# A three-layer decoder block on one core: VectorE's chains cut into single steps, and every engine's call list written anew

## The reference, cut to what matters

```python
x = _layernorm(x + attn(x))            # a state-space mixer: x @ W_in, a 4-tap causal
                                       # convolution, silu, decay matrices, gate, W_out
x = _layernorm(x + xattn(ctx, x))      # 8 heads of 64; keys are the 120 context rows
                                       # and the 256 own rows, 376 in all
x = _layernorm(x + ffn(x))

def ffn(x):
    gf = global_net(x.mean(axis=1, keepdims=True))
    out = x
    for _ in range(3):
        tf = coupling_net(out)         # three gelu layers and a sigmoid
        coupling = 0.1 + adaptive_range * (0.7 * gf + 0.3 * tf - 0.5) * 2
        out = out + coupling * twist(out)
    return out
```

## Time and profile before

| | |
|---|---|
| median of 3 runs | 3865.07 us (3864.32 to 3865.35) |
| span of the profiled execution | 3861.4 us |
| device time of the profiled execution | not given apart from the span; the span lies 3.7 us under the median |
| TensorE busy | 3783.3 us, 98% |
| VectorE busy | 3286.2 us, 85% |
| ScalarE busy | 3237.9 us, 84% |
| GpSimd busy | 1748.5 us, 45% |
| transfers | 203.14 MB, mean 53 GB/s |

### The profile page before, as it was taken

One profiled execution on the slowest core, in us unless ns is written; L12 is line 12 of the kernel. 1 busy time (PEld: TensorE's weight loads), 2 busy tenths in 40 slices (PEclk: granted clock), 3 DMA queues, 4 the chain that ended last, 5 costly groups with the idle time before them and its releaser, 6 DMA issues.

```text
span 3861.4 us, 77375 instructions
## 1 busy us (share of the span) xinstructions
PE 3783.3 (98%) x25728; PEld 3000.9 (78%) x25728; DVE 3286.2 (85%) x8098; ACT 3237.9 (84%) x7812; POOL 1748.5 (45%) x3084
## 2 busy tenths in 40 slices
PE   6999999999999999999999999999999999999997
PEld 5777877877877878778778778777787787787775
DVE  7888888888888888888888888888888888888874
ACT  5788888888888888888888888888888888888885
POOL 3444445354454444453544544534535445445442
PEclk8999999999999999999999999999999999999998
DMA  3111112111211111121111111111211211111110
GB/s 97 54 47 59 55 45 61 54 42 58 58 45 55 48 59 54 45 61 53 43 57 59 45 55 50 56 55 45 61 55 42 61 55 45 55 54 53 55 38 17
DMA packets 312350, 203.14 MB, mean 53 GB/s; under 512 B 55056, under 2 KB 310928, under 8 KB 311952
## 3 DMA queue, kind: packets, MB, share of 16 engines
q1 hardware_dynamic: 311952, 198.20, 17.5%
HBM read 180.17 MB, written 17.96 MB: 51 GB/s over the span
## 4 chain that ended last, share of the span: by engine, by line
PE 59%; ACT 16%; DVE 15%; issue 4%; POOL 4%; DMA 1%; SPq 0%; DVEq 0%; POOLq 0%
PE psum L253 20%; PE psum L428 8%; PE psum L338 6%; PE psum L463 5%; PE psum L438 5%; PE psum L452 4%; PE psum L325 4%; ACT prob L979 3%; ACT h L1021 2%; ACT L979 2%; ACT L1021 2%; PE psum L497 2%; ACT xc L891 2%; POOL rs_mix L2175 2%; DVE nmax L1638 1%
## 5 line engine op out<-in xcount | busy, mean ns | idle before, releaser
L979 ACT ACTIVATE prob<-psum,nmax 128x376 f32<-128x376 f32 x1024 | 585.2, 575 | 49.5 <-DVE nmax L1638 46.2
L1638 DVE TENSOR_REDUCE nmax<-psum 128x1 f32<-128x376 f32 x1024 | 541.5, 540 | 14.4 <-PE psum L428 11.0
L2139 POOL TENSOR_TENSOR Lm<-Lm,G 128x384 f32<-128x384 f32 x512 | 506.1, 1012 | 92.8 <-DVE out_sb L1741 68.4
L438 PE MATMUL psum<-ident,prob 128*128 128x128 f32 (+1 forms) x3072 | 480.5, 276 | 2.1 <-ACT probT L989 1.1
L1442 DVE SCALAR_TENSOR_TENSOR u<-psum,par,u 128x253 f32<-128x253 f32 (+5 forms) x960 | 449.1, 479 | 28.1 <-ACT u L882 1.7
L428 PE MATMUL psum<-kT,q_sb 64*128 64x376 f32 x2048 | 467.7, 528 | 0.2 <-ACT prob L979 0.2
L438 PEld LDWEIGHTS psum<-ident,prob 128*128 128x128 f32 (+1 forms) x3072 | 363.0, 141 | 73.9 <-issue 45.0
L989 ACT ACTIVATE probT<-psum 128x384 f32<-128x384 f32 x512 | 252.7, 494 | 182.7 <-PE psum L438 182.5
L2126 POOL TENSOR_SCALAR_AFFINE_SELECT Lm<-Lm 128x256 f32<-128x256 f32 x512 | 205.7, 435 | 411.6 <-DMA Lm<-cum_row 411.6
L253 PE MATMUL psum<-x_hi,w_in_hi 128*128 128x256 f32 (+1 forms) x1152 | 360.9, 313 | 22.5 <-DVE w_in_lo L1764 9.3
L452 PE MATMUL psum<-probT,V 128*64 128x256 f32 (+1 forms) x3072 | 375.0, 385 | 0.3 <-ACT probT L989 0.3
(11 more groups left out here) (222 smaller groups left out, 11157.9 us busy)
## 6 DMA issues: line engine op xcount, KB each, us to landing
Lm<-cum_row SPq DMA_DIRECT2D x64, 1024.0 KB, 5.2
Lm<-cum_row SPq DMA_DIRECT2D x64, 512.0 KB, 6.5
invT<-inv_row SPq DMA_DIRECT2D x256, 128.0 KB, 3.0
xT_sb<-in_xT SPq DMA_DIRECT2D x64, 256.0 KB, 3.1
x_sb<-in_x SPq DMA_DIRECT2D x64, 256.0 KB, 3.3
result<-out_sb SPq DMA_DIRECT2D x64, 256.0 KB, 2.2
inv_row<-inv_t SPq DMA_DIRECT2D x512, 1.0 KB
ctx_sb<-in_ctx SPq DMA_DIRECT2D x64, 120.0 KB, 2.7
```

Of the source, the lines that this page charges most:

```text
L438: t = tr(banks[b][0:m, j * P:(j + 1) * P], prob[:, r, j0:j0 + m], ident[:, :])
L979: act(prob[:, r, :], b[:, 0:NK], ACT.Exp, bias=nmax[:, n:n + 1], accum_out=psum_row[:, n:n + 1]).then_inc(a_exp, 1)
L1638: e.tensor_reduce(nmax[:, n:n + 1], banks[bank_of["sc", s, n]][:, 0:NK], AX.X, ALU.max, negate=True).then_inc(d_max, 1)
L2139: t = tt(Lm[:, h, :], Lm[:, h, :], G[:, :], ALU.mult)
```

## The change

All five engines' lists are drawn up anew, for the prologue, the loop and the tail. The instructions that compute are the same, and as many on TensorE. On VectorE the helpers that held several dependent steps are divided into helpers of one step each, and steps of different chains alternate: `taps` becomes `tap`, `bc` becomes `bc_silu`, `bc_high` and `bc_low`, `cum` three calls, `x1_raw` three calls per half, `kv_split`, `x2_split`, `inverse`, `norm`, `cycle` and `out_sum` likewise. The convolution gets one semaphore for each of its four row blocks in place of one. The bank of `bcdt` is now freed by two semaphores in place of one. The core of it:

```diff
-            def taps(src, c, rows, done, at):
-                for n, d in enumerate((1, 2, 3)):
+            def tap(src, c, rows, n, done, s):
+                d = n + 1
+                ve.wait_ge(done, 3 * s + n)
                     stt(u[0:rows, c, d:L], src[:, 0:L - d], prm("conv_w", 4 * c + 3 - d, slice(0, rows)),
                         u[0:rows, c, d:L], ALU.mult, ALU.add).then_inc(done, 1)
-                    if n < 2:
-                        ve.wait_ge(done, at + n + 1)
...
-                freed[b] = [(d_dta, s + 1)]
+                freed[b] = [(d_dta, s + 1), (d_uB, 3 * s + 3)]
...
-                freed[b] = [(d_u, 12 * s + 6 * j + 6)]
+                freed[b] = [(d_u[2 * j], 3 * s + 3), (d_u[2 * j + 1], 3 * s + 3)]
...
-            def out_sum(s, i):
+            def out_x(s, i):
...
+            def out_tw(s, i, k):
...
-            def cycle(s, cyc):
+            def gain(s, cyc):
...
+            def twisted_part(s, cyc):
...
+            def pre(s, cyc):
```

More of the change, by code:

```diff
@@ L573, in _ @@
+            k_tile(0, 0)
+            k_tile(0, 1)
+            scores(0, 0, 0)
+            xcT(1, 0)
+            in_z(1, 0)
+            k_tile(0, 2)
+            xcT(1, 1)
+            v_tile(0, 0)
+            scores(0, 0, 1)
+            cb(1)
             in_z(1, 1)
             q_pair(0, 1)
[L575 to L581 removed]
             turn(0, 0)
+            scores(0, 1, 0)
@@ L739, in _ @@
+            x1T(last)
+            twisted(last - 2)
             turn(last - 1, 8)
+            layer(last - 2, 0, 3)
+            glob(last - 2, 2)
             turn(last - 1, 9)
-            glob(last - 2, 2)
-            twisted(last - 2)
-            turn(last - 1, 10)
-            x1T(last)
-            layer(last - 2, 0, 2)
+            scores(last - 1, 3, 0)
+            values(last - 1, 0)
+            values(last - 1, 1)
             scores(last - 1, 3, 1)
-            layer(last - 2, 0, 3)
@@ L772, in _ @@
+            values(last - 1, 2)
+            values(last - 1, 3)
+            scores(last, 0, 1)
+            v_tile(last, 0)
+            layer(last - 2, 2, 3)
+            w_o(last - 1, 0)
+            w_o(last - 1, 1)
+            scores(last, 1, 0)
+            turn(last, 0)
             q_pair(last, 1)
-            layer(last - 2, 2, 3)
+            scores(last, 1, 1)
             turn(last, 1)
-            scores(last, 1, 1)
+            x2_turn(last - 1)
+            k_tile(last, 3)
+            scores(last, 2, 0)
@@ L776, in _ @@
             turn(last, 2)
+            v_tile(last, 1)
+            scores(last, 2, 1)
             turn(last, 3)
-            scores(last, 2, 0)
-            k_tile(last, 3)
             turn(last, 4)
-            scores(last, 2, 1)
-            x2_turn(last - 1)
-            v_tile(last, 0)
+            glob(last - 1, 0)
+            layer(last - 1, 0, 0)
+            v_tile(last, 2)
+            scores(last, 3, 0)
             turn(last, 5)
-            glob(last - 1, 0)
-            scores(last, 3, 0)
```

1804 lines of the change are left out of this document (1048 added, 756 removed).

## The result

| | before | after |
|---|---|---|
| median | 3864.7 us (3864.0 to 3865.35) | 4159.2 us (4152.5 to 4163.5, 4 runs) |
| ratio | | 1.076, 95% interval 1.0744 to 1.0775 |
| span of the profiled execution | 3861.4 us | 4161.6 us (device time 4163.5 us) |

The kernel after takes 295 us more. The forecast was 3842 us, its range 3808 to 3880.

A forecast was written before the change was run, and what follows sets the result against it. TensorE, busy 3783.3 of 3861.4 us, was taken as the bound. Loop -0.4 us per iteration times 61 = -24.4, start +3, end -1 gave 3839 us of span; with 3.7 added, 3842 us was forecast, range 3808 to 3880.

The forecast's parts named there:

- term 3: New TensorE waits in the loop, mainly turn(a, 0) behind x2_raw: +0.5 us per iteration (0 to +1.4).
- term 2: TensorE waits in the loop that go, for a gelu, x_lo and small overruns: -0.45 us per iteration (0 to -0.85).
- new waits outweigh: Rival: x2_raw behind the output sums delays TensorE, up to 1.4 us per iteration; 3885 to about 3897 us; chance 0.14.
- Term 1: TensorE's array shape in the loop: four fewer whole-to-half round trips, three more direct half changes, -0.45 us per iteration.
- a wait behind `x2_raw` over 0.9 us: Sign that the forecast is wrong: TensorE's wait behind x2_raw exceeds 0.9 us.
- a gelu's wait that grew: Sign that the forecast is wrong: TensorE's wait for a gelu at the layers grows; no size given.
- Term 4: VectorE's alternating single steps save it some 3 us of 51 per sequence, but 0 of kernel time, TensorE being the bound.
- Term 5: The start: weights and context load placed differently delay the first xcT some 6 us; steady pipeline +3 us (-3 to +8).
- Term 6: The end, one sequence's chain in the last 62 us: -1 us (-3 to +3).
- The eighth table load: Rival: ScalarE's added 1.28 us load before a layer's gelu leaves TensorE waiting; 3858 to 3901 us; chance 0.03.

The follow-up runs named there:

- Experiment 6: Kernel after with VectorE's bc_high, bc_low and x1_keep (2.4 us) moved from ahead of pre to behind it: 4120.0 us, ratio 1.0658 to the kernel before.
- Experiment 1: Kernel after with GpSimd's factors of the output sum no longer waiting for the next sequence's division: 4052.5 us, ratio 1.0487 to the kernel before.
- experiment 9: Kernel before with only the convolution taps of two row blocks alternating, a semaphore for each block: 3861.6 us, ratio 0.9992.
- experiment 2: Kernel after with GpSimd's twist call ahead of the four masked calls instead of behind them: 4123.5 us, ratio 1.0667 to the kernel before.
- Experiment 7: Kernel after with the factors not waiting for the division, and bc_high, bc_low and x1_keep behind pre: 4021.4 us, ratio 1.0402 to the kernel before.
- experiment 12: About 50 loop calls moved to other places by a calculation, in each kernel: before 3876.5 us (1.0034), after 4054.6 us (1.0488).
- experiment 11: Kernel after with the prologue's weights(0, 3) and weights(0, 4) late and SP's context load early, as before the change: 4154.8 us, ratio 1.075 to the kernel before.
- experiment 5: Kernel after with four edits: factors free of the division, twist before masks, spread_inv before loads, two decays behind the copies of oT: 4086.6 us, ratio 1.0576.

## Why the prediction was wrong

**The step that failed is term 3, waits that come: +0.5 per iteration, at most 1.4.** Over the 60 full distances between `x2_turn` calls TensorE is idle for 4.5 us per iteration in place of 0.3: 4.2 us more. Three things in the step were wrong.

*It looked at the wait in the place where I found one, and not at the list in front of each use.* The largest wait stands at `layer(f, 2, 1)`, for which term 2 said that TensorE's cover was "about as much as now" and gave a gain of 0.1. What I didn't add up was VectorE's list between the last copy and `pre`: 11.1 us, and 1.1 more to the gelu's result, against 9.1 us of work on TensorE. Had `bc_silu` taken its old 0.8 us in place of 3.0, 10.0 us would still have stood against 9.1. Experiment 6 shows the cause of this wait: take 2.4 us out, and 109 us of it are gone. The new lists had it all; I counted what TensorE has ahead of its wait, but not what VectorE has ahead of its answer.

*The chain behind the division was the right one, its length and its start were not.* From the second division to `x2_raw` I had 5.2 us; measured 2433.14 - 2427.01 = 6.1. The wait came where it was put (59 times), with 1.04 us in place of 0.35: the chain was 0.9 us longer, 0.97 and 0.74 us for steps that I had at 0.35, beside GpSimd. The forecast's bound (0.8) was passed. And the division itself waits 5.0 us on VectorE, for the sums and for ScalarE, which moves VectorE's whole list. Experiment 1 puts the factors' wait for the division at 107 us, 1.75 us per iteration, 66 of them idle time. The rival "new waits outweigh" named this mechanism, and its point of 0.95 us was passed (by its own sum it is 1.0: 0.9 for terms 1 and 2, 0.1 to pass 3872.8), but its upper price, 1.4, was a third of the 4.2 that came, and more than half of that stands at places that it does not name. Two of the prediction's signs of being wrong came with it: a wait behind `x2_raw` over 0.9 us, and a gelu's wait that grew.

*Prices that depend on a neighbour were taken as fixed.* VectorE's busy time was to fall to 3100 us and rose to 3310: the steps saved by alternating (32 us for the taps, experiment 9) are less than what `bc_silu` alone gained beside GpSimd (58.7 + 85.0 us for its two lines where they took 26.1 + 26.7). The wait at `xcT` (0.87 us per iteration) is due to this; it went when `twist` did (experiment 2). The lower clock behind a stall, some 0.7 us per iteration, was in no term.

The rest by its own steps. **Term 1**, -0.45: too large. Experiment 7 has TensorE's list of after with the lower clock nearly gone. Over the 60 full distances between `x2_turn` calls TensorE is busy for 58.7 us per sequence before, 59.2 after, and 58.5 in experiment 7. The gain is about 0.2 us, near my lower bound. A round trip costs more (0.39) than I took (0.15), so four fewer would be 1.6; that only 0.2 of it is seen would mean, as an estimate, that each of the 3 more changes from one kind of half to the other costs about 0.45, where I took 0.05, or that other costs of the order make up for it. By these two prices the orders of experiment 12 (2 round trips more and 1 direct change fewer, each against its own kernel) should cost 0.3 us; measured were 0.5 and 1.4. So the shapes account for most of the first and for little of the second; what the rest is stays open. **Term 2**: the 4.0 us at `x_lo` went, as said (it waits once, at the start); the gelu's 0.19 became 1.85. **Term 4**, nothing: right, measured at 0.9992. The prediction set the page "VectorE: DVE Perf Modes" of the Trainium skill (The DRAIN you can't avoid) against its rows. Experiment 9 bears the rows out, 2.42 us in place of 2.94 for six taps; and the section says too that a next operation which isn't held starts earlier, so read in full it isn't against them. **Term 5**, +3 with bounds to +8: measured 11.8. Its step at `xcT` was right (7.6 us later where it had 6, and due to the weights and the context load, experiment 11); what it left out is the order of the other calls. **Term 6**, -1: measured +1, in its bounds. **The eighth table load**: ScalarE's busy time rose to 3321 us (3316 forecast), and no wait of TensorE stands at the layer behind it.

The sum, from what was measured: 4.2 idle + 0.7 lower clock (59.2 - 58.5) - 0.2 shapes (58.7 - 58.5) = 4.7 us per iteration, against 4.75 seen. Halving the 89 us at the lower clock gives much the same for the second term, 44 us or 0.8 per iteration.

**What stays open.** With two edits, 138 of 295 us are taken back; at that point TensorE still waits 2.9 us per iteration at `cb`, `xcT`, `w_o` and `out_proj`, each 0.2 to 1.1. That they are interlocked is shown by how badly the gains in idle time add (experiments 5 and 6). Which order would free them all, what made the orders of experiment 12 dearer beyond their shapes, what made TensorE's busy time longer in experiment 5, and why some stalls bring the lower clock and others don't, is not settled.

## What to carry to other kernels

When lists are redrawn, follow each answer back on the engine that gives it: add up all that this engine has in its list between the last thing it could only do after TensorE's previous step and the answer, and set it against TensorE's work in the same stretch. Here one such sum, 12.2 us against 9.1, was worth more than all the terms of the forecast. A kernel at 98% on one engine has 2% of waiting to win by order and far more to lose, so where the stretches are not added up the range belongs mostly above. And a wait that has been taken away is worth its time only if the next place where the lists meet has slack; of 109 us at one wait, 39 came out, and only 13 of those as idle time. Look at idle time and busy time apart before a gain is put down to a wait.

## What the hardware showed that I had not expected

- VectorE instructions with two inputs in SBUF took 1.42 to 1.57 us in place of 0.40 to 0.42, and 0.97 in place of 0.35, while a GpSimd instruction ran. All 108 `bc_silu` instructions of the kernel after that took over 0.7 us ended 0.27 to 0.28 us behind the end of a GpSimd instruction.
- After 1.8 us without work in an otherwise busy stretch, TensorE's granted clock was at its lower level for about 3.4 us. Where the waits were 1.1 us and less on average (experiment 7) it was there for 3 us between 200 and 3800 us, not 89. With the same waits of 1.8 us but none behind `x2_raw` (experiment 1) it was 27 us, so the length of one stall doesn't decide it alone.
- Two more round trips of the array from whole to half and back cost 0.39 us each, and they count as busy time.
- The same products in another order without any idle time cost 0.5 us more in 59; with 2 round trips more and 1 direct change fewer, some 0.3 of it is the shapes, as an estimate.
- Six dependent taps on VectorE took 2.94 us in a row and 2.42 when two chains alternated.
